# Disentangled attention on one Trainium2 core: position tables by row bands from projected queries and keys, near terms by two engines, first biases copied on chip, later batches prepared inside the score loop

## The reference, cut to what matters

```python
q = split_heads(x @ Wq + bq); k = split_heads(x @ Wk + bk); v = split_heads(x @ Wv + bv)
scores = einsum('bhqd,bhkd->bhqk', q, k) / scale
pos_k = (rel_embeddings @ Wk + bk)                       # 64 positions, split in heads
c2p = take_along_axis(einsum('bhqd,hpd->bhqp', q, pos_k), clip(rel + 32, 0, 63), -1)
p2c = take_along_axis(einsum('bhkd,hpd->bhkp', k, pos_k), clip(-rel + 32, 0, 63), -1)
probs = softmax(scores + (c2p + swapaxes(p2c)) / scale)  # rel: log-bucketed query - key
out = layernorm((probs @ v) @ Wo + bo + x)
```

## Time and profile before

| | us |
|---|---|
| three runs | 753.46, 753.55, 755.36 (median 753.55) |
| span of the profiled execution | 752.3 |
| first FFN, to its last scatter | 0 to 122.3 |
| block change and opening, to the first added score | 122.3 to 166.5 |
| score loop, to the last sub-step | 166.4 to 455.1 |
| second FFN, splines, causal attention, splines | 455.1 to 752.3 |

### The profile page before, as it was taken

How to read it: one execution, slowest core, us unless ns; L and a number is a source line. 1 busy time by engine, 2 the same in 40 slices (tenths; PEclk the granted TensorE clock), 3 DMA queues, 4 the chain that set the end, 5 groups by cost and what they waited for, 6 DMA issues and landing times. The chain is left out here.

```text
span 752.3 us, 17249 instructions
## 1 busy us (share of the span) xinstructions
PE 581.5 (77%) x5361; PEld 417.1 (55%) x5361; DVE 532.0 (71%) x1881; ACT 453.5 (60%) x983; POOL 203.6 (27%) x262
## 2 busy tenths in 40 slices
PE   4399993079999999999899998452996673678780
PEld 3288883045666666767576766341985342346450
DVE  7543320967787788999799995873224799867897
ACT  3245562047888888999799996550552534376723
POOL 1745332401912720660400000043443200211200
PEclk9999998589999999999999999655998787799985
DMA  8878567699899999999744421833554000000001
GB/s 241 221 240 289 181 215 205 212 300 331 242 349 330 296 313 309 255 251 345 185 136 141 134 65 22 238 86 127 170 180 121 2 1 0 0 1 1 1 1 56
DMA packets 130378, 127.80 MB, mean 170 GB/s; under 512 B 27962, under 2 KB 108002, under 8 KB 129394
## 3 DMA queue, kind: packets, MB, share of 16 engines
q1 hardware_dynamic: 122722, 99.85, 46.7%
q0 software_dynamic: 3920, 25.26, 8.8%
q10 hardware_dynamic: 3648, 1.59, 0.8%
HBM read 68.37 MB, written 48.79 MB: 156 GB/s over the span
## 5 line engine op out<-in xcount | busy, mean ns | idle before, releaser
L1714 DVE CUSTOM_DVE_ANT_0 l0am_prob<-l0am_ps_s,l0am_bias 128x512 f32<-128x512 f32 x256 | 166.6, 689 | 33.8 <-PE l0am_ps_s L1788 24.1
L1631 ACT ACTIVATE l0am_prob<-l0am_prob,l0am_neg_top 128x512 f32<-128x512 f32 x256 | 171.4, 723 | 6.8 <-DVE l0am_neg_top L1714 6.8
L1801 PE MATMUL l0am_ps_t<-c_ident,l0am_prob 128*128 128x128 f32 x1024 | 129.0, 275 | 0.4 <-DVE l0am_probT L1701 0.4
L1801 PEld LDWEIGHTS l0am_ps_t<-c_ident,l0am_prob 128*128 128x128 f32 x1024 | 110.9, 141 | 16.5 <-issue 8.0
L636 ACT ACTIVATE l0f_h<-l0f_psU,l0f_experts 128x128 f32<-128x128 f32 x212 | 60.7, 369 | 83.0 <-PE l0f_psU L962 82.9
L829 DVE COPY l0f_xsT<-l0f_psT 128x128 f32<-128x128 f32 x53 | 15.4, 291 | 99.0 <-PE l0f_psT L952 99.0
L1701 DVE COPY l0am_probT<-l0am_ps_t 128x512 f32<-128x512 f32 x128 | 82.2, 684 | 1.4 <-PE l0am_ps_t L1801 1.4
L1788 PE MATMUL l0am_ps_s<-l0am_ks,l0am_qs 32*128 32x512 f32 x512 | 74.4, 651 | 3.5 <-DVE l0am_neg_top L1714 2.6
L1625 ACT COPY l0am_probT<-l0am_ps_t 128x512 f32<-128x512 f32 x128 | 68.5, 589 | 10.7 <-PE l0am_ps_t L1801 10.7
L531 POOL DMA_INDIRECT token_results<-l0f_ys,l0f_token_i x53 | 51.1, 965 | 78.3 <-DVE l0f_ys L839 75.0
L1815 PE MATMUL l0am_ps_cg<-l0am_probT,l0am_v 128*9 128x128 f32 x2048 | 68.7, 275 | 2.7 <-DVE l0a_heads L1725 2.7
(11 more groups left out here) (340 smaller groups left out, 949.6 us busy)
## 6 DMA issues: line engine op xcount, KB each, us to landing
l0am_bias<-near_terms SPq DMA_DIRECT2D x128, 192.0 KB, 4.6
near_terms<-l0am_near POOLq DMA_DIRECT2D x6, 3072.0 KB, 12.3
l0f_mine<-l0f_experts SPq DMA_DIRECT2D x53, 256.0 KB, 2.4
near_terms<-l0am_near SPq DMA_DIRECT2D x4, 1536.0 KB, 7.5
l0o_rows_k<-position_k SPq DMA_DIRECT2D x12, 512.0 KB, 6.9
l0f_experts<-in_L_ffn_w SPq DMA_DIRECT2D x2, 2048.0 KB
l0f_experts<-in_L_ffn_w SPq DMA_DIRECT2D x16, 256.0 KB
position_q<-l0o_rows SPq DMA_DIRECT2D x16, 256.0 KB, 4.3
```

What stands on the lines that cost most here:

```text
L1631: nc.scalar.activation(prob[:, k, :], prob[:, k, :], ACT.Exp, bias=neg_top[:, k:k + 1], scale=-1.0)\
L1714: dve.tensor_tensor_reduce(out=prob[:, k, :], in0=ps_s[:, j, :], in1=bias[:, j, at:at + S], scale=-1.0, scalar=HUGE, op0=ALU.add, op1=ALU.min,
L1801: last = pe.transpose(ps_t[:, BANK_OF[j], i, :], prob[:, u % SLOTS_, i * P:(i + 1) * P], ident[:, :])
```

## The change

1. **Tables.** `extend` and `wext` go. The first batch's queries and keys are projected (`project`, two full products) and kept in SBUF as `qk`; row products are made from them in bands of 32 rows (`multiply`: 8 for each batch instead of 10 full products), two at a time into two PSUM banks, one copied by ACT and one by DVE. `multiply_bias` is two matmuls at slot 12. The rows of the first batch are loaded by 8 DMAs instead of 32.
2. **Near terms of batch 0.** DVE adds the corners and 21 bands, POOL the other 11.
3. **First biases.** The eight loads of group 0 become 32 copies of one partition of `near` each into 64 partitions of `bias` (28 issued by SP, 4 by ACT); ACT clears `bias` instead of POOL.
4. **Later near stores.** A group's 32 partitions are now four runs of 8 neighbours, each stored by a DMA of its own, all by POOL.
5. **Later batches.** Turning, projecting, row products and values of batches 1 to 3 stand in the score loop (`LATE_STEPS`, 20 quads). POOL brings in the results of batches 2 and 3. The roots of the variances come from ACT's Ln and Exp.
6. **Quads.** DVE copies its two turned probabilities in one instruction; `close_heads` goes ahead of the four additions and one quad later; PE turns the heads behind the probabilities. POOL no longer waits for the last scatters at the end of the FFN: SP and ACT do in the next block.

```diff
+LATE_STEPS = {0: [("turn", 1), ("project", 1)], 5: [("values", 1)],
+              7: [("turn", 2)], 8: [("project", 2)], 13: [("values", 2)],
+              17: [("turn", 3)], 18: [("project", 3)], 23: [("values", 3)]}
+LATE_STEPS |= {first + n: [("rows", BATCH_ROWS * b + 2 * n)] for b, first in ((1, 1), (2, 9), (3, 19)) for n in range(QUARTERS)}
+FIRST_DVE_RUNS = RUNS_OF[0] + RUNS_OF[1] + RUNS_OF[2][3:]
+FIRST_POOL_RUNS = RUNS_OF[3] + RUNS_OF[2][:3]
...
     def multiply(self, pe, cn, banks):
...
+        for n, bank in enumerate(banks):
+            r = slice(32 * (first + n), 32 * (first + n) + 32)
+            pe.matmul(bank, self.aside.spread[r, side, :], self.qk[r, side, :], start=True, stop=True,
+                      tile_position=(32 * (first + n), 0)).then_inc(self.tab_psum, 1)
...
+            def first_bias(queue, t, halves):
+
+                for s in halves:
+                    for j in range(GROUP):
+                        p, at = NB * GROUPS * j + 2 * t + s, NEAR_AT[t] + 64 * s
+                        queue.dma_start(bias[64 * s:64 * s + 64, j, at:at + WIN],
+                                        near[p:p + 1, :].rearrange("p (q w) -> p q w", w=WIN)).then_inc(bias_in[t], 16)
...
-                store_first_near(0)
...
+                sp.wait_ge(near_dve, 1)
+                sp.wait_ge(near_pool, 1)
+                first_bias(sp, 0, (0,))
+                for t in range(1, T4):
+                    first_bias(sp, t, (0, 1))
...
+                    for j in range(GROUP):
+                        p = NB * (GROUPS * j + g)
+                        pool.dma_start(bass.AP(dram["near"].tensor, (b * P + p) * part, [(part, NB), (1, part)]),
+                                       near[p:p + NB, :]).then_inc(near_out[g], 16)
...
                 for q in range(QUADS + 4):
                     if 2 <= q < QUADS + 2:
-                        copy_turned(4 * (q - 2) + 2)
-                        copy_turned(4 * (q - 2) + 3)
+                        copy_last_two(q - 2)
+                    if 4 <= q:
+                        close_heads(q - 4)
                     if q < QUADS:
                         add_terms(4 * q)
                         add_terms(4 * q + 1)
-                    if 3 <= q < QUADS + 3:
-                        close_heads(q - 3)
```

More of the change, by code:

```diff
@@ L440, in load_results @@
                     .then_inc(gathered[b], 16)
-        with nc.Block() as block:
+        with nc.Block(no_gpsimd_drain=opening is not None) as block:
             @block.sync
@@ L1162, in copy_bias, with multiply_bias @@
+                n0 += n
+        last.then_inc(self.spread_ready, 1)
+    def multiply_bias(self, pe):
+        pe.wait_ge(self.spread_ready, 1)
+        for side in range(2):
+            last = pe.matmul(self.ps[:, 0, side * QUARTERS:(side + 1) * QUARTERS], self.spread[:, side, :], self.less_near[:, :],
+                             start=True, stop=True)
+        last.then_inc(self.bias_psum, 1)
     def copy_bias(self, act):
         act.wait_ge(self.bias_psum, 1)
-        self.nc.scalar.copy(self.row_bias[:, :], self.ps[:, 0, 0:BATCH_CHUNKS]).then_inc(self.wext_ready, 1)
@@ L1428, in near_build, with near_bands @@
[L1428 to L1430 removed]
+            return last
+        def near_bands(engine, runs):
+            for d0, d1, pq, _ in runs:
+                at, width, r = 64 - d1, d1 - d0 + 1, ROW_OF[pq]
+                last = engine.tensor_tensor(
+                    view(near, at, (WIN + 1, 64), (1, width)), view(rows_q, r * 64, (1, 64), (0, width)),
+                    view(rows_k, r * NARROW + at - NARROW_AT[r], (1, 64), (1, width)), ALU.add)
+            return last
@@ new lines, in _ @@
+                nc.scalar.preload_act_table_set("natural_log_exp_and_others")
+                for out, count in opening.results_out:
+                    act.wait_ge(out, count)
+                nc.scalar.activation(bias[:, :, :].rearrange("p j (k d) -> p (j k) d", d=D),
+                                     c["blank"][:, 0:1, 0:D].broadcast_to((P, GROUP * BIAS_COLS // D, D)), ACT.Identity).then_inc(filled, 1)
+                act.wait_ge(filled, 1)
+                act.wait_ge(near_dve, 1)
+                act.wait_ge(near_pool, 1)
@@ new lines, in wait_late_copies @@
+                def wait_late_copies(pe, q, by_act):
+                    for kind, what in LATE_STEPS.get(q, ()):
+                        if kind == "turn" and not by_act:
+                            pe.wait_ge(xT_ready, what + 1)
+                        elif kind == "project":
+                            pe.wait_ge(*((opening.q_ready, what + 1) if by_act else (opening.k_ready, what + 1)))
+                        elif kind == "rows":
+                            pe.wait_ge(opening.rows_by_act if by_act else opening.rows_by_dve, what // 2 + 1)
+                        elif kind == "values" and not by_act:
+                            pe.wait_ge(v_ready, what + 1)
```

788 lines of the change are left out of this document (382 added, 406 removed).

## The result

The changed kernel took 1018.38 us (median of 4 runs, 1014.42 to 1024.45) against 753.5 for the kernel before on the same chip: ratio 1.3511, interval 1.3452 to 1.357. It is slower by a third, where 723 was forecast.

A forecast was written before the change was run, and what follows sets the result against it. PE bounds the score loop (busy 283.92 of 288.70 us); ahead of it, SP's row loads, then DVE's near terms. 752.3 - 24.5 (opening) - 3.8 (plain quads) - 2 (slow quad) = 722, plus 1.25: 723 us; range 707 to 757.

The forecast's parts named there:

- At 7.5 it costs nothing: Later near stores in the loop: a group's store takes 7.5 us, so POOL's 53 us per batch fit in 72.
- the 14.7 at which the text put the loss of the whole gain: Later near stores: at 14.7 us per group store (107 GB/s), three batches' lateness loses the whole gain of 30.
- Slower: few partitions give little rate: Rival on near stores and first copies: rate goes with how partitions lie; 757 to far over 900 us, chance 0.17.
- FFN, last scatter from 122.3 to 114: Opening FFN: bias matmuls save 3 us, row products 5.6, so the last scatter moves from 122.3 to about 114.
- SP's end at 114.8, block at 116: Opening: 24 fewer row loads at 0.64 save 15.4 us; SP's issue ends near 114.8, the new block starts near 116.
- Near terms at 135: Batch 0's near terms, split between DVE and POOL, end at 135, between 131 side by side and 137 in turn.
- the 137 priced by it: End of batch 0's near terms by the skill's contention rule: 137 instead of 135, two microseconds more.
- First biases, 7.2: Copies of the first biases: 2.6 us of issues and 4.6 of landing, first addition 7.2 us behind the near terms.
- First addition from 166.5 to 142, by the near terms and biases: Opening up to the loop's first score addition: near terms at 135 plus 7.2 give 142, a gain of 24.5 us.
- Plain quads, -3.8: Score loop: moving the heads' division gives 0.06 us for each of 63 intervals, -3.8; bounds 0 and -10.
- Late quads, 0: Score-loop quads with later batches' products: 24 times 0.94 us before and after, so 0; between -6 and +5.
- Slow quad, -2: The one 7.05 us quad, 2.9 over plain: smaller near stores leave room between, giving back 2 us.

The follow-up runs named there:

- run 1: Changed kernel with each near store of 4 x 8 partitions replaced by one of 128 partitions, first copies kept: 808.87 us, 1.0754 of the kernel before.
- run 3: Changed kernel with near stores of 128 partitions and first biases by way of DRAM instead of one-partition copies: 792.75 us, 1.0537 of the kernel before.
- run 4: Kernel before, later near stores waited for singly in three forms (8 neighbours, 32 neighbours, 32 partitions four apart): 886.0 us, 1.1766.
- run 8: Kernel before with 8 row loads instead of 32 for batch 0, its group stores reading 32 neighbouring partitions: 757.95 us, 1.0069.
- run 10: Kernel before, with POOL neither waiting for its last results nor draining at the FFN's end: 751.38 us, 0.9993.
- run 7: Kernel before, its first store and eight bias loads replaced by 32 one-partition copies, all by SP, no near store beside them: 767.41 us, 1.0188.
- run 12: Kernel before without POOL's wait and drain at the FFN's end, SP issuing the last 12 of 32 row loads first in the next block: 745.6 us, 0.9894.
- run 9: As run 3, with the near stores of batches 1 to 3 left out: 756.8 us, 1.0066 of the kernel before.
- run 6: As run 3, with each later batch's near store in two pieces, the second issued after the first landed: 795.49 us, 1.0566 of the kernel before.

## Why the prediction was wrong

The step that failed is "At 7.5 it costs nothing", the price of the near stores. It took the row of a store from 32 partitions four apart for stores from 8 neighbours, though the earlier trace rows spoke against it. From the first of batch 1's 16 stores to the scores that could go on behind them 85 us passed, 21 for a group, beyond the 14.7 at which the text put the loss of the whole gain. Of the 265 us between the two kernels, 209.5 went with the form of the stores (run 1), 16 with the copies beside wide stores (run 3), and 39 with the rest of the change.

The rival "Slower: few partitions give little rate" is what happened; its mechanism is shown by runs 1 and 4, and 0.17 was too little for it. What even the rival lacked: it counted only the lateness of the stores' own readers, which at 21 us a group makes about 106 us by its own sum, while the loop lost 231. SP's rows, stacks, tiles and biases stand behind the same stores (83.5 us for a bias piece), so each edge loses more than its store is late.

The other steps:

- *FFN, last scatter from 122.3 to 114*: 121.33 (121.32 before). The 3 us of the bias matmuls came: slot 16 begins at 76.40, not 79.28. They went again in slots 23 to 28. A pair of 32-row products, priced at half of a full one, costs more than one: a slot with such a pair lasts 3.15 (98.34 to 101.48), a slot with a full product before 2.75, and a quad with a pair 5.38 (226.01 to 231.39), a late quad before 5.09. And DVE's copy of the last row pair waits for a row store, with the slot's turned tokens behind it on DVE, which the sum had not seen:

```profile
76.40 0.33 PE L960 MATMUL l0f_psT<-c_ident,l0f_xs 128*128 128x128 f32 x1 [1.19 <-DMA l0f_xs<-sorted_tokens]
109.83 0.75 DVE L1288 TENSOR_SCALAR l0o_rows<-l0w_ps,l0w_row_bias 128x512 f32<-128x512 f32 x1 [4.32 <-DMA position_q<-l0o_rows]
110.83 1.16 PE L970 MATMUL l0f_psU<-l0f_xsT,l0f_mine 128*128 128x128 f32 x8 [1.89 <-DVE l0f_xsT L835]
```

- *SP's end at 114.8, block at 116*: 120.98 and 122.25. The last rows were copied 9 us earlier than before (110.58, not 119.44), but SP took 9.7 us for the eight loads (111.30 to 120.98), 1.2 each and not 0.64: each has four times the partitions, and from 112 to 121 the DMA engines were full (share 1.04, before 0.67). The sum also put the block's end on SP alone; runs 8 and 10 show two holders, of which either alone keeps it, and here POOL's last scatter ends at 122.29.
- *Near terms at 135*: 142.8. DVE's bands start 3.7 later than counted (127.75, not 124.0) and last 15.07, where even one engine after the other made 13.0. The 21 bands took 0.72 us each instead of 0.32. They stood beside POOL's 11 and, from 137 on, beside four more additions of POOL, those of batches 2 and 3 that the prediction hid in a later slack:

```profile
137.01 2.13 POOL L1191 TENSOR_TENSOR l0a_heads<-l0a_heads,l0o_half_gate 128x512 f32<-128x512 f32 x2
139.22 2.66 POOL L1197 TENSOR_TENSOR x_tokens<-x_tokens,l0a_heads 128x512 f32<-128x512 f32 x2
```

  There a DVE band of 128x128 took up to 1.36 us, 0.29 before. The Trainium skill's rule ("SBUF — State Buffer", "Who interferes with whom") names the right pair of engines; the 137 priced by it fell 6 short, 3.7 of them by the late start.
- *First biases, 7.2*: 60.5. Without stores beside them a copy takes 0.97 of SP's queue (run 7), which 4.6 us of landing for all of them did not allow for; with wide stores beside them the wait was 27.4 (run 1), and the rest came with the narrow form. Run 3 bounds what the copies cost beside wide stores: 16 us.
- *First addition from 166.5 to 142, by the near terms and biases*: in the kernel before, the first addition waits for PE, not for its biases, over a chain whose end the prediction did not name (near terms, normalising, values, scores); run 12 moves it as a whole. In the changed kernel PE's work for the later batches stands in the loop, PE begins the first scores at 138.73, and the biases come last.
- *Plain quads, -3.8*: 4.15 as before. PE is the whole quad; the division's place gave nothing.
- *Late quads, 0*: dearer. In run 3 the 19 late quads behind the first took 28.2 us over the plain price, from score to score, where 24 x 0.94 = 22.6 were counted: +5.6, a little past the bound of +5.
- *Slow quad, -2*: the opposite. The later near stores, even wide and in pieces, cost 36 us at their new time (run 9). Preparing the batches inside the loop starts their rows, and so their near terms, too late ahead of the quad that reads them; run 6 excludes that the four-at-once issue is to blame, and no run moved the builds earlier, so the lead itself is argued from the times of run 3 and not shown.

The range missed because it was built from the opening's and the loop's own rows and left the one unpriced transfer outside.

## What to carry to other kernels

Price a DMA by which partitions it touches, not by its bytes alone: a split that makes stores smaller can make the same bytes several times slower (44 against 239 GB/s in run 4), and transfers queued beside it lose time too. Where a block ends at a barrier, look for a second engine that ends as late before you count a gain from the first. Two engines on one elementwise job can end later than one of them alone; count with the rate that each has beside the other, and with all that the second engine does at that time.

## What the hardware did that I had not expected

- POOL's narrow stores held SP's queue: a single issue on SP lasted up to 47.54 us while POOL's 16 stores were under way, with the DMA engines only 42% busy at 88 GB/s.
- 21 additions of two SBUF tables on DVE took 15.07 us beside 11 and then four more of POOL, and 32 took 10.35 alone.
- A copy out of one partition (48 KB) costs 0.97 us of the issuing queue with no near store beside it (run 7), 1.7 (48.58 / 28) beside wide stores and 2.8 (77.79 / 28) beside narrow ones.
- A block change with POOL's wait and drain stood 9.16 us behind its last scatter (run 8); without them 1.82 (run 12).
